# Weight tile 3 summed before the gates of the second layer 1, weight tests moved, low parts ahead of totals

## The reference, cut to what matters

```python
x = x + _L0_xattn_ref(_layernorm(x), ctx, ctx, ctx)   # gelu(x ctx^T) * (x ctx^T) ctx
x = x + _L0_ffn_ref(_layernorm(x), w1, w2, h1, h2, w3)
...
def _L0_ffn_ref(x, ...):
    h = silu(tlin(x, w1_w, w1_s)) * tlin(x, w2_w, w2_s)
    h = gelu(tlin(h, h1_w, h1_s), approximate=False)
    h = gelu(tlin(h, h2_w, h2_s), approximate=False)
    return tlin(h, w3_w, w3_s)          # tlin: (x w^T) * s
```

## Time and profile before

| | us |
|---|---|
| median of 3 runs (lowest, highest) | 358.19 (357.68, 358.39) |
| the profiled execution, its time | 359.3 |
| its span, first to last instruction | 357.5 |
| TensorE busy | 328.7 (92%) |
| VectorE busy | 275.4 (77%) |
| ScalarE busy | 218.4 (61%) |
| mean granted TensorE clock | 0.976 of 2.4 GHz |

### The profile page before, as it was taken

The page is one execution under the profiler, slowest core; times in us unless marked ns, Lnnn a source line. Parts: engine busy times, 40 slices in busy tenths (PEclk is TensorE's granted clock), DMA queues, the critical chain, the costliest instruction groups (busy, mean ns, idle before and its releaser), DMA issues.

```text
span 357.5 us, 4797 instructions
## 1 busy us (share of the span) xinstructions
PE 328.7 (92%) x1636; PEld 273.9 (77%) x1636; DVE 275.4 (77%) x508; ACT 218.4 (61%) x367; POOL 33.5 (9%) x64
## 2 busy tenths in 40 slices
PE   7799999508999999999999999999998999999995
PEld 5589888307886888888987787687886788888894
DVE  3596998980899588987677848769898876878784
ACT  2447557340469664787833539576959777577860
POOL 6131020000010001300420000200000000000000
PEclk9999999957999999999999999999999899999999
DMA  5899496379997965454300532356285286584003
GB/s 162 263 347 380 176 312 239 76 264 372 397 330 223 314 213 178 143 190 138 117 2 29 206 107 87 114 184 242 69 319 177 57 330 227 175 251 138 0 2 124
DMA packets 24173, 68.61 MB, mean 192 GB/s; under 512 B 1744, under 2 KB 3152, under 8 KB 21456
## 3 DMA queue, kind: packets, MB, share of 16 engines
q1 hardware_dynamic: 16656, 49.37, 39.3%
q0 software_dynamic: 7488, 18.88, 17.5%
HBM read 57.75 MB, written 10.49 MB: 191 GB/s over the span
## 4 chain that ended last, share of the span: by engine, by line
PE 72%; DVE 13%; DMA 5%; issue 4%; ACT 4%; POOL 1%; DVEq 0%; SPq 0%; ACTq 0%; POOLq 0%
PE P L1310 52%; PE P L1262 8%; PE P L1339 8%; DMA blocks_h<-H 2%; DVE H L890 2%; PE P L1218 2%; DVE TR L917 2%; PE P L1226 2%; DMA WR<-blocks_h 1%; DMA xn<-in_w 1%; PE P L1234 1%; DVE xt L939 1%; DVE st L809 1%; DVE H L912 1%; DVE H L933 1%
## 5 line engine op out<-in xcount | busy, mean ns | idle before, releaser
L1310 PE MATMUL P<-TR,WR 128*128 128x512 f32 x896 | 209.4, 395 | 16.3 <-DMA WR<-blocks_h 14.2
L1310 PEld LDWEIGHTS P<-TR,WR 128*128 128x128 f32 x896 | 169.4, 190 | 54.1 <-DMA WR<-blocks_h 14.6
L917 DVE TENSOR_TENSOR TR<-H,TR 128x512 fp32r<-128x512 f32 x112 | 75.8, 688 | 34.7 <-ACT TR L618 32.8
L618 ACT ACTIVATE TR<-H 128x512 fp32r<-128x512 f32 x112 | 68.4, 626 | 25.0 <-DVE H L912 22.4
L1262 PE MATMUL P<-X,W 128*128 128x512 f32 (+1 forms) x320 | 63.1, 352 | 1.1 <-DVE X L879 0.6
L1262 PEld LDWEIGHTS P<-X,W 128*128 128x128 f32 x320 | 51.6, 189 | 9.8 <-DVE X L879 1.0
L632 ACT ACTIVATE H<-P 128x512 f32<-128x512 f32 x48 | 27.8, 595 | 32.7 <-PE P L1310 32.7
L912 DVE TENSOR_TENSOR H<-H 128x512 f32<-128x512 f32 x64 | 42.1, 686 | 0.3
L890 DVE SCALAR_TENSOR_TENSOR H<-P,sc,SLY 128x512 f32<-128x512 f32 (+1 forms) x40 | 25.2, 639 | 16.9 <-ACT SLY L608 9.2
L654 ACT ACTIVATE H<-H,sc 128x512 f32<-128x512 f32 x40 | 28.2, 720 | 14.8 <-DVE H L933 14.8
L608 ACT ACTIVATE SLY<-P,sc 128x512 f32<-128x512 f32 (+1 forms) x40 | 23.7, 599 | 17.7 <-PE P L1262 16.7
(11 more groups left out here) (77 smaller groups left out, 211.3 us busy)
## 6 DMA issues: line engine op xcount, KB each, us to landing
WR<-blocks_h SPq DMA_DIRECT2D x16, 1024.0 KB, 6.2
WR<-in_h POOLq DMA_DIRECT2D x12, 1024.0 KB, 6.2
H<-in_h SPq DMA_DIRECT2D x5, 1024.0 KB, 16.8
blocks_h<-H SPq DMA_DIRECT2D x5, 1024.0 KB, 5.8
xn<-in_h SPq DMA_DIRECT2D x8, 512.0 KB, 3.6
xt<-in_h SPq DMA_DIRECT2D x8, 512.0 KB, 3.7
W<-in_w POOLq DMA_DIRECT2D x4, 512.0 KB, 6.1
X<-in_h POOLq DMA_DIRECT2D x2, 1024.0 KB, 6.7
```

The lines of the kernel that those rows point to most:

```text
L618: eng.activation(TR[:, f % RING, 0, :], operand(c, L, s, kk), ACT.Copy).then_inc(s_hi, 1)
L917: eng.tensor_tensor(TR[:, f % RING, 1, :], operand(c, L, s, kk), TR[:, f % RING, 0, :].bitcast(f32), ALU.subtract).then_inc(s_lo, 1)
L1310: out_ = eng.matmul(bank(c, L, s, m)[:, :], WR[r % WRING][:, at:at + 128], TR[:, f % RING, h, :], start=(s in FRESH[L] and kk == 0 and h = ...
```

## The change

- **Sums.** `combine(3)` moves from `layer1(1)` at m = 5 into `early_products(0)`, behind `combine(2)`. In the odd tiles' `layer1` the adds stand one or two gates later (m = 2 to 5, before 0 to 3), `lo` at m = 4 to 7, and ACT's `hi` at m = 3 to 6 (before 1 to 4). `combine(4)` stays at m = 7.
- **SP's queue.** `sums_out(4)` and `load_raw(6)` stand ahead of `load_sum(0, 0, 3)`; `sums_out(5)` and `(6)` one place earlier.
- **Tests.** Four semaphores and, for later tests, four places (`tested`): tests 0 to 5 use `SL` and `Y` and stand beside chunk 0 (4 in stage (0, 1, 6), 5 behind the first `lo4` loop), 6 to 9 use `xn[0]` and `xt`, and 10 to 21 take the four in turn. In chunk 1 none is left in `layer1(2)` and `early_products(1)`; 6, 7, 8 are in `layer1(3)`, 9 to 12 in `late_products(1)`, 13 to 19 in `square(1)`, and 20 and 21 behind its `lo4` loop, `BESIDE4`. The first gate of tile 2 waits for six tests, and `last` of half 1 for 6 (chunk 0) or all 22 (chunk 1).
- **Rests ahead of totals.** `late_products` does four `lo(6)` and then four `total`, before one by one; ACT's four `hi(6)` come before its gelus.
- **Beside layer 4 of chunk 0.** `weigh` one k earlier, `turn(1, 4)` and `(1, 5)` one k earlier, `resid(4)` and `(5)` together at k = 4 and the scales at k = 6 (before 1, 3 and 4, 5); two table copies on ACT between the last `hi4`; `stats(0, 6)` and `(0, 7)` in stages 4 and 5 of `square(0)`, before both in 6. In `layer1(2)` the turns and scores stand one group later.

```diff
-            if t == 1 and m in (5, 7):
-                combine(3 + m // 6)
+            if (t, m) == (1, 7):
+                combine(4)
...
             if c == 0:
                 combine(2)
-            else:
-                test(7)
+                combine(3)
...
+        BESIDE4 = {0: (5,), 1: (20, 21)}
...
+            load_check(4)
+            load_check(5)
...
             add_up(c, 0, 4)
             if c == 0:
                 combine(7)
-            else:
-                test(BESIDE[1, 0, 3])
+            for i in range(4):
+                lo(c, 0, 6, i)
             for i in range(4):
                 total(c, 0, (0, 1), i)
-                lo(c, 0, 6, i)
...
             for k in range(4, 8):
                 lo4(c, 1, k)
+            for n in BESIDE4[c]:
+                test(n)
...
-            if c == 0 and s == 6:
-                stats(0, 6)
-                stats(0, 7)
+            if c == 0 and s in (4, 5):
+                stats(0, 2 + s)
...
-                if (half, k) == (1, 7):
+                if (half, k) == (1, 6):
                     weigh(4)
                     weigh(5)
-                if (half, k) == (0, 6):
+                if (half, k) == (0, 5):
                     turn(1, 4)
                     turn(1, 5)
```

More of the change, by code:

```diff
@@ L128, in xattn_ffn @@
         s_v = [sem(f"s_v{i}") for i in range(WRING)]
-        s_chk = [sem("s_chk0"), sem("s_chk1")]
+        s_chk = [sem(f"s_chk{i}") for i in range(4)]
         s_id, s_one, s_mh, s_ve = sem("s_id"), sem("s_one"), sem("s_mh"), sem("s_ve")
@@ L679, in late_products @@
                     hi(c, 0, 2, i)
-                    if i == 2 and (c, 0, 1) in BESIDE:
-                        magnitude(BESIDE[c, 0, 1])
+                    if i == 2:
+                        for n in beside(c, 0, 1):
+                            magnitude(n)
                 for s, nxt in ((2, 3), (3, 4)):
@@ L685, in late_products @@
                         hi(c, 0, nxt, i)
-                        if i == 2 and (c, 0, s) in BESIDE:
-                            magnitude(BESIDE[c, 0, s])
+                        if i == 2:
+                            for n in beside(c, 0, s):
+                                magnitude(n)
                 for i in range(4):
                     hi(c, 0, 6, i)
+                for i in range(4):
                     gelu(c, 0, (0, 1), i)
@@ L692, in late_products @@
                     hi(c, 1, 0, i)
+                for n in beside(c, 0, 6):
+                    magnitude(n)
                 for i in range(4):
                     gelu(c, 0, (1, 1), i)
-                if c == 1:
-                    magnitude(BESIDE[1, 0, 4])
-                    magnitude(BESIDE[1, 0, 6])
             def square(c):
@@ L716, in square @@
                             hi4(c, 1, i)
-                        if i == 2 and (c, 1, s) in BESIDE:
-                            magnitude(BESIDE[c, 1, s])
+                        if i == 2:
+                            for n in beside(c, 1, s):
+                                magnitude(n)
             eng.wait_ge(s_mh, 1)
@@ L761, in _ @@
                         gelu(c, 1, (1, 0), i)
+                    if c == 0 and i >= 2:
+                        copy_t(2 + i)
+                for n in BESIDE4[c]:
+                    magnitude(n)
                 if c == 0:
-                    copy_t(4)
-                    copy_t(5)
                     gelu(0, 1, (1, 0), 2)
@@ L972, in square @@
                                 lo4(c, 1, i - 1)
-                    if (c, 1, s) in BESIDE:
-                        test(BESIDE[c, 1, s])
+                    for n in beside(c, 1, s):
+                        test(n)
                     if c == 0 and s == 2:
@@ L989, in late_products @@
                     combine(5)
-                else:
-                    test(BESIDE[1, 0, 1])
+                for n in beside(c, 0, 1):
+                    test(n)
                 for i in range(4):
@@ L997, in late_products @@
                     combine(6)
-                else:
-                    test(BESIDE[1, 0, 2])
+                for n in beside(c, 0, 2):
+                    test(n)
                 add_up(c, 0, 4)
@@ L1012, in late_products @@
                     lo(c, 1, 0, i)
-                if c == 1:
-                    test(BESIDE[1, 0, 4])
-                    test(BESIDE[1, 0, 6])
+                for n in beside(c, 0, 6):
+                    test(n)
             def early_products(c):
@@ L1060, in last @@
                     eng.wait_ge(s_s3, 16)
-                    eng.wait_ge(s_fl, 4)
+                if half == 1 and q == 0:
+                    eng.wait_ge(s_fl, (6, TESTS)[c])
                 if q == 0:
```

113 lines of the change are left out of this document (60 added, 53 removed).

## The result

| | before | after | ratio, 95% interval |
|---|---|---|---|
| median, us (lowest to highest; 4 runs each) | 358.29 (357.68 to 358.55) | 340.78 (339.99 to 342.38) | 0.9519 (0.948 to 0.9559) |
| the profiled execution, its time / its span | 359.3 / 357.5 | 339.99 / 338.2 | |
| TensorE busy | 328.7 (92%) | 323.6 (96%) | |
| mean granted clock | 0.976 | 0.997 | |

In the changed kernel `product` is L1328, layer 4 is L1357, layer 1 is L1280, a `total` L954, `lo` L938, `lo4` L944, a test L960, `magnitude` L580, `sums_out` L352, `load_raw` L347, `load_sum` L363.

What follows compares the result with a forecast made beforehand. TensorE, busy 92%, was held mainly by a 14.2 us wait for the first summed weights before product (0, 0, 1). Terms -11.0 - 1.05 - 3.2 - 0.6 - 3.4 + 2.6 = -16.65; 358.2 - 16.65 = 341.5 us, range 338.0 to 347.5.

Steps and rivals of the forecast that it cites:

- A: Chunk 0 to product (0, 0, 6): earlier sum removes the 14.2 us stall, product starts at 101.5 instead of 112.5, -11.0 us.
- B: Layer 4 of chunk 0: layer 1 of tile 2 starts at 192.65 instead of 193.71, -1.05 us.
- C: Layer 1 of tile 2 until that of tile 3: small gaps shrink with later turns and no tests, -3.2 us.
- D: Layer 1 of tile 3: tests moved to m = 1, 2 and 7, VectorE ahead at the end, -0.6 us.
- E: Product (1, 0, 6): its 1.69 us wait for VectorE and the 1.7 us clock loss go, -3.4 us.
- F: Kernel end: tests 19, 20 and 21, new there, delay the last lo4 and final operations, +2.6 us.
- the read of sum 4: Before product (0, 0, 4): lands at 93.5 beside POOL's load, TensorE wants it at 90.0, a 3.5 us wait.
- 0.7 for the clock: In A: the wait for read 4 may lower the clock; 0.7 us added, between nothing and 1.7.
- rival 2: VectorE alone bounds chunk 0, reads in time, no clock fall, turns not late: 338.8 us, chance 15%.
- Rival 1: Weights bound chunk 0, both waits lower the clock, product 6 at 104 to 105: 346.2 us, chance 25%.
- Rival 4: Slower: crowded sums of h2 delay load_sum(0, 1, 1) behind 128; at 132 it takes 362 us, chance 2%.
- The rule of the Trainium skill: Repeated transfer waits can each drop the clock; charging those at 67 and 90 costs 2.7 us more than the sum.

Runs made afterwards that it cites:

- after_again: The changed kernel as it is, run once more: 340.83 us.
- a_read4: The changed kernel with the read of sum 4 issued ahead of the write of sum 5 in SP's queue: 341.19 us.
- a_sum_late: The changed kernel with combine(3) put back at m = 5 of layer1(1), all else as changed: 353.25 us.
- a_test_back: The changed kernel with test 11 back before the totals of chunk 1's layer 1, rests and totals one by one in both chunks: 342.02 us.
- a_rests_back: The changed kernel with rests and totals one by one again in both chunks, also hi(6) and gelus on ACT: 341.37 us.
- b_sum_alone: The kernel before with only combine(3) moved behind combine(2): 347.9 us.
- a_all: The changed kernel with total(1,1) before total(0,1), read of sum 4 before write of sum 5, tests spread from chunk 1's start: 338.53 us.

## Why the prediction was right, point by point

The forecast was 341.5 (338.0 to 347.5); measured 340.78. Its terms against the segments of the two profiled executions, from the starts of the rows above and of the earlier trace rows:

| | segment | before | after | measured | forecast |
|---|---|---|---|---|---|
| A | to product (0, 0, 6) | 112.48 | 99.36 | -13.1 | -11.0 |
| B | to layer 1 of tile 2 | 81.2 | 80.2 | -1.0 | -1.05 |
| C | to layer 1 of tile 3 | 37.5 | 34.5 | -2.9 | -3.2 |
| D | to the products of chunk 1 | 15.15 | 14.5 | -0.6 | -0.6 |
| E | to layer 4 of chunk 1 | 90.95 | 87.2 | -3.7 | -3.4 |
| F | to VectorE's last end, and out | 20.2 | 22.4 | +2.1 | +2.6 |
| | sum | 357.5 | 338.2 | -19.3 | -16.65 |

- **A, too small by 2.1, and outside its ends (-12.5).** The mechanism was right: the sum is written early, the read lands 0.6 us after TensorE is free (product (0, 0, 1) at 67.7, forecast 68.1), then VectorE and the weights nearly together. Three sizes were off. The step that failed most is the read of sum 4: it was put at 93.5, which is 90.5 by the count of transfers and 3 us for the company of POOL's load, and landed at 91.2 (issued at 79.3, 11.9 us), so the company cost 0.7. The prediction's own sign, a wait of 2 to 4 us there, did not come (1.54), nor its 100 to 102 for product (0, 0, 6). Then 0.7 for the clock, taken between nothing and 1.7: in this execution it stayed at 1.00 from 68 to 99. In the profile of after_again the wait at product 4 was 1.79 and the clock did fall behind it; there layer 4 began at 158.75 instead of 157.87. The square products had begun together (67.67 and 67.68), and 0.25 of the 0.88 is the later read (product 4 at 91.52 instead of 91.27). So the fall costs some 0.6 us and not 1.7: it takes up the wait for VectorE at product 6, which is not there any more. And VectorE's total ended at 99.2, not 99.9, 0.2 of it because the adds began at 70.94. With the wait for the read at 1.54, VectorE is the last at product 6 by 0.55, which is what a_read4 shows; rival 2 (VectorE alone) was nearer there than the forecast.
- **B, right in sum**, and made of smaller parts than told: the turns waited 0.30 and 0.47, where 0.5 and 0.7 stood.
- **C and D** as forecast (the products of chunk 1 began at 246.3 before). They were read off the gaps of before, and no run took them apart. a_sum_late shows that they do not hang on A, and that all that is not A gives 4.9 us together by the medians, against 6.2 by the segments. Part of the difference is in E.
- **E, right, for half of the reasons given.** The test between third rest and totals makes the wait (a_test_back); the rests one by one alone don't (a_rests_back). In the square layers of chunk 1 the clock was 1.00 in both profiles of the changed kernel. But nearly half of E, the 1.7 us for the clock (the row has 0.72 where the prediction reads 0.71), may be lost only in some executions of the kernel before: b_sum_alone has the same wait of 1.69 us there and the clock at 1.00 behind it (the last section has its row).
- **F, right but for 0.5.** TensorE waited 0.79 (0.85 told), and the four final operations, which need not wait for TensorE any more, follow one another at 0.79 us and not 0.9.
- **The sum.** The segments miss the forecast by 2.7 us, the medians by 0.7. The other 2 us lie between the executions: the forecast took off the 1.1 by which the profiled execution of before exceeds its median, and the executions of after differ by more than those of before (spans of 337.9 to 341.1 in the set of after_again, at clocks of 1.0 to 0.994; before, in the same set, 355.8 to 357.4 at 0.979 to 0.974). So the nearness of 341.5 to 340.78 is in part luck; -16.65 against -17.5 is what the work was good for.
- **Rival 1** (the weights bound, with the clock) had product (0, 0, 6) at 104 to 105; it came at 99.4, and the wait at product 4 was 1.54. **Rival 4** lives on in small: not the read for the second layer but the load of test 0 behind it is what the landing of the last sum holds up, by 0.58 us in the changed kernel and 3.28 in a_all.
- **The clock.** The rule of the Trainium skill that the prediction weighed ("TensorE: Matmul & The Clock Gate", "HAM oscillation — how this bites in real kernels") was taken there to charge both waits in chunk 0. What the page tells of is a loop with waits several times as long as the one at 67 us (0.57, or none), which was followed by no fall in either profile of the changed kernel; the one at product 4 was followed by none after 1.54 us and by one after 1.79. So at these two places in two executions the trace has one fall, and that cost 0.6 us of the 2.7 that the prediction took from the rule.

## What to carry to other kernels

When a stall of TensorE is taken away, two things come due at once: the work that the engine beside it caught up during the stall, and the transfers that had time until then. Work out both dates, since the later one sets the gain; mending one of two that lie a microsecond apart gives little (here +0.4 and -0.9 us, against -1.9 for both). Small work moved into free places is free only where the chain of engines has slack: in stages that are full a lag of 2 us stays, 47 us on, and a stage can be full though no engine in it is. And an order that is changed for one wait is best changed only in the loop that has the wait: by the profiles, the same swap in the other chunk used up the gain, which no run has tested.
